# Second stage: down weights of the experts issued by ScalarE on its own DMA queue

## The reference

```
q_emb = relu(cond @ W3 + b3)
h     = relu(((64 * x + sum_over_tokens(x)) * q_emb) @ W2 + b2)
shared = (silu(h @ sw_gate) * (h @ sw_up)) @ sw_down       # inner width 2 * 352 = 704
scores = softmax(h @ gate_w.T); top 6 of 64 experts for each token
each expert takes at most 64 tokens (the first 64 in token order):
    y = (silu(g @ w_gate[e]) * (g @ w_up[e])) @ w_down[e]  # 512 -> 352 -> 512
out   = x + shared + sum over a token's experts of y * score
```

## Time and profile before

| | |
|---|---|
| median of 3 runs | 1211.64 us (1211.52 to 1211.75) |
| profiled execution | 1211.44 us |
| its span | 1209.6 us |
| TensorE busy | 1204.5 us |
| VectorE busy | 857.4 us |
| ScalarE busy | 329.9 us |
| GpSimd busy | 272.9 us |
| DMA, 700 to 800 us | 0.92 of the 16 engines' time, 302 GB/s |
| granted TensorE clock | 1.00 |

### The profile page before, as it was taken

The page is one execution under the profiler, slowest core; times in us unless marked ns, Lnnn a source line. Parts: engine busy times, 40 slices in busy tenths (PEclk is TensorE's granted clock), DMA queues, the critical chain, the costliest instruction groups (busy, mean ns, idle before and its releaser), DMA issues.

```text
span 1209.6 us, 15909 instructions
## 1 busy us (share of the span) xinstructions
PE 1204.5 (100%) x5705; PEld 889.3 (74%) x5705; DVE 857.4 (71%) x1868; ACT 329.9 (27%) x631; POOL 272.9 (23%) x246
## 2 busy tenths in 40 slices
PE   9999999999999999999999999999999999999998
PEld 8888888888888888888866666666666666666666
DVE  7998989988888898886656555664655664655652
ACT  4454243434324353343111111110111201111111
POOL 0000000000000000000136245263463553543421
PEclk9999999999999999999999999999999999999999
DMA  9946444372643626246767988989989889899863
GB/s 220 223 111 192 96 135 118 92 179 52 179 103 85 174 75 158 56 141 200 244 222 248 333 278 271 338 280 276 338 260 327 299 284 307 292 304 301 275 145 87
DMA packets 158999, 250.91 MB, mean 207 GB/s; under 512 B 22664, under 2 KB 93704, under 8 KB 157768
## 3 DMA queue, kind: packets, MB, share of 16 engines
q1 hardware_dynamic: 142528, 222.22, 58.3%
q0 software_dynamic: 14048, 25.18, 10.5%
q10 hardware_dynamic: 2344, 2.50, 0.7%
HBM read 197.14 MB, written 61.10 MB: 213 GB/s over the span
## 4 chain that ended last, share of the span: by engine, by line
PE 95%; DVE 3%; issue 0%; ACT 0%; DMA 0%; DVEq 0%; ACTq 0%
PE bank L1509 23%; PE bank L1510 22%; PE bank L1511 22%; PE bank L1713 13%; PE bank L1728 7%; PE bank L1535 2%; PE bank L1632 1%; PE bank L1631 1%; PE bank L1569 1%; PE bank L1567 1%; PE bank L1580 1%; PE bank L1638 0%; DVE x L951 0%; DVE xpart L955 0%; DVE x L968 0%
## 5 line engine op out<-in xcount | busy, mean ns | idle before, releaser
L1509 PE MATMUL bank<-hh,gu 128*128 128x512 f32 x704 | 278.0, 395 | 0.0
L1510 PE MATMUL bank<-hl,gu 128*128 128x512 f32 x704 | 274.2, 390 | 0.0
L1511 PE MATMUL bank<-hh,gu 128*128 128x512 f32 x704 | 274.1, 389 | 0.0
L629 POOL DMA_INDIRECT hg<-table,idx_quarter x128 | 126.5, 988 | 643.5 <-DVE idx_hi L1391 594.0
L1509 PEld LDWEIGHTS bank<-hh,gu 128*128 128x128 f32 x704 | 132.2, 188 | 39.1 <-issue 12.8
L1511 PEld LDWEIGHTS bank<-hh,gu 128*128 128x128 f32 x704 | 132.2, 188 | 27.8
L1510 PEld LDWEIGHTS bank<-hl,gu 128*128 128x128 f32 x704 | 132.2, 188 | 26.2
L697 ACT ACTIVATE ah<-prod 128x512 fp32r<-128x512 f32 x96 | 60.6, 632 | 302.6 <-DVE prod L1051 287.2
L1468 DVE STREAM_TRANSPOSE eactT<-eact 32x96 f32<-32x96 f32 (+1 forms) x512 | 133.9, 261 | 7.9
L1509 PE MATMUL bank<-sdh,ah 128*128 128x512 f32 x320 | 125.9, 393 | 0.0
L1510 PE MATMUL bank<-sdl,ah 128*128 128x512 f32 x320 | 124.6, 390 | 0.0
(11 more groups left out here) (132 smaller groups left out, 1672.8 us busy)
## 6 DMA issues: line engine op xcount, KB each, us to landing
wg<-in_L_ffn_w_gate_dram SPq DMA_DIRECT2D x64, 704.0 KB
wu<-in_L_ffn_w_up_dram SPq DMA_DIRECT2D x64, 704.0 KB
wd<-in_L_ffn_w_down_dram SPq DMA_DIRECT2D x64, 512.0 KB
table<-hrow SPq DMA_DIRECT2D x64, 256.0 KB, 4.3
x<-in_x_dram SPq DMA_DIRECT2D x60, 256.0 KB, 6.8
wd<-in_L_ffn_w_down_dram SPq DMA_DIRECT2D x64, 192.0 KB
out_dram<-outst SPq DMA_DIRECT2D x35, 256.0 KB
outst<-in_x_dram SPq DMA_DIRECT2D x32, 256.0 KB, 3.5
```

What stands on the lines that cost most here:

```text
L629: nc.gpsimd.indirect_dma_start(out=hg[p % 3][:, b, :], out_offset=None, in_=quarters, in_offset=bass.IndirectOffsetOnAxis(ap=idx_quarter[: ...
L1509: nc.tensor.matmul(o, st_h, mv_h, start=first_mm, stop=False)
L1510: nc.tensor.matmul(o, st_h, mv_l, start=False, stop=False)
L1511: return nc.tensor.matmul(o, st_l, mv_h, start=False, stop=last_mm)
```

## The change

ScalarE issues the down weights of units 1 to 31, on its own queue, after the same semaphore as before and ahead of the SiLU of the unit. SP keeps the down weights of unit 0 (in the first stage, unchanged) and issues gate, up and h as before, on the first queue. Buffers, sizes and semaphores are the same.

```diff
@@ SP's block
-            def load_down(p):
-                wait(sp, s.edown_filled, p)
+            def load_first_down():
                 for e in range(2):
-                    src = w_down[p + NP * e]
+                    src = w_down[NP * e]
                     sp.dma_start(wd[e][:, 0:IT - 1, :],
                                  src[0:(IT - 1) * P, :].rearrange("(i p) d -> p i d", p=P)).then_inc(down_in[e], 16)
                     sp.dma_start(wd[e][0:ITAIL, IT - 1, :], src[(IT - 1) * P:I, :]).then_inc(down_in[e], 16)
...
-            load_down(0)
+            load_first_down()
...
-                if kind == "experts" and 0 < n < NP:
-                    load_down(n)
                 if kind == "experts" and n + 2 < NP:
                     load_gate(n + 2)
                     load_up(n + 2)
@@ ScalarE's block
+            def load_down(p):
+                act.wait_ge(s.edown_filled, p)
+                for e in range(2):
+                    src = w_down[p + NP * e]
+                    act.dma_start(wd[e][:, 0:IT - 1, :],
+                                  src[0:(IT - 1) * P, :].rearrange("(i p) d -> p i d", p=P)).then_inc(down_in[e], 16)
+                    act.dma_start(wd[e][0:ITAIL, IT - 1, :], src[(IT - 1) * P:I, :]).then_inc(down_in[e], 16)
...
                 if kind == "experts" and n < NP:
+                    if n > 0:
+                        load_down(n)
                     silu_expert(n)
```

## The result

The changed kernel takes 1225.53 us (median of 6 runs, 1220.8 to 1231.71), the kernel before 1211.68 (6 runs, 1211.48 to 1212.0). The ratio is 1.0115, 95% interval 1.0083 to 1.0147: slower, by 13.9 us, where 1224.8 had been forecast. The runs spread over 11 us, where the six of before spread over 0.5 us and the 20 that were run beside the first experiments over 2.5 us (1211.27 to 1213.75).

A forecast was written before the change was run, and what follows sets the result against it. TensorE, almost never idle, was taken as the bound. Late down weights in two backlog and six short units add 13.2 us to 1211.44, giving 1224.6, or 1224.8 as median; own range 1215 to 1238, with rivals 1211.3 to 1242.

The forecast's parts named there:

- TensorE has no slack: Whole span: TensorE is busy for all but 5 us of 1209.6, so late weights lengthen the run directly.
- Issuing costs nothing on ScalarE: Four DMA issues ahead of each unit's SiLU: 0 us taken, bounds 0 to 28; up matmuls cover any delay.
- Turns by packet: DMA engines alternate queues per packet; 2 KB down rows beside 5.6 KB rows get about 30% of the time.
- short units: Six units with about 15.8 us between down phases: down weights late by 1.3 us each, bounds 0 and 3.
- GpSimd's store often runs then: In short units the accumulating store adds 19 x 0.17 us, landing at 13.4 us against 13.1 available.
- the working: Down-weight landing from packet turns on a mean engine: 10.2 us after issue usually, 13.4 with the store.
- the last of 16 comes about 1 us later: End of a down transfer: the slowest DMA engine finishes about 1 us after the mean one, an estimate.
- The backlog: Two units issued while large packets still queue: down weights late by 2.7 us each, bounds 0 and 6.
- The sum: Total lateness of down weights over the run: 2 x 2.7 + 6 x 1.3 = 13.2 us, bounds 0 to 30.
- Rival 2: GpSimd's serial scatters, slowed by a third queue, become the bound: +28 us, 1239; chance 0.09 as main term.

The follow-up runs named there:

- the first experiment: Changed kernel with the order restored: SP issues gate and up weights only after the unit's down weights landed, both queues kept; 1212.07 us, ratio 1.0002.
- the exchange: Kernel before, with gate and up weights of units 2 to 31 moved to ScalarE's queue instead of the down weights; 1226.09 us, ratio 1.0115.
- the down-last kernel: Kernel before, one queue, SP issuing each unit's down weights after the gate and up weights of unit n + 2; 1360.53 us, ratio 1.1239.
- the cut store: Changed kernel with GpSimd's two accumulating stores of a chunk's shared part cut from 256 to 32 rows each; 1212.16 us, ratio 1.0008.
- the 4 KB rows: Changed kernel with 256 of each down matrix's 352 rows loaded as 128 pieces of 4 KB instead of 256 of 2 KB; 1216.38 us, ratio 1.004.
- the half-row kernel: Changed kernel with each gate and up matrix loaded in 2.8 KB pieces instead of 5.6 KB, by two DMAs; 1218.28 us, ratio 1.0066.

## Why the prediction was right

- *TensorE has no slack*: right. Waits and clock account for 17.2 of 17.35 us.
- *Issuing costs nothing on ScalarE*: right for the time. The four took from 752.73 to 755.19 in the changed kernel and the SiLU began at 755.29; all on ScalarE gave 1211.73.
- *Turns by packet, for SP's and ScalarE's queues too*: right. That the two kinds of weights must not overlap is shown by the restored order and by the exchange; that they share by turns and not by bytes, by the packet size on either side. The turns are what the Trainium skill, DMA: Bandwidth & Descriptors, section Queues, rings and completion order, states. On its 9 to 17 descriptors in a packet the prediction argued from the equal counts of rows 6; that does not hold, as equal groups on both sides would give equal counts too. The packet records at the end of the unit that landed at 963.85 do tell: its last rows begin in pairs at 961.95, 962.2, 962.5 and 962.8, one about each 0.3 us and not in bursts, which is one row of each queue in turn (0.094 + 0.22).
- *Where*: right in kind (short units and the backlog), wrong in number. Six short units late by 1.3 us were forecast; the trace has three, by 1.3, 4.8 and 1.0 us. Two steps failed. "GpSimd's store often runs then" holds for two of six (in two more it ends within 2.4 us of the issue), and the store was priced too low: the working gives it 19 turns (13.4 us after the issue), but at 834.32 it was issued together with the down weights of 835.01 and ran beside them until 852.1, and they landed after 17.7 us. And "the last of 16 comes about 1 us later" was mis-sized: rows 10, from which it was taken, give 2.4 us (6.5 against 4.1), and in the third late unit, with no store to speak of, the end of the transfer made all of the lateness, landing 14.0 us after the issue where 10.2 was worked out for a mean one. That these add up to 7.1 us against 7.8 is luck.
- *The backlog*: two units of 2.7 us were forecast, one of 4.8 was found (issue 769.94, landed 790.38, so 20.4 us where the working had 17.5 to 18.5). This too comes near by luck: one unit for two, at nearly twice the lateness. The other followed the long wait at 848 to 853, and the time lost there gave its transfer room (852.86 to 873.75).
- *The sum*: 11.9 us of waits against 13.2. That the median came within 1 us of 1224.8 owes much to luck, since a term was missing that is not small: the clock after long waits, 5.3 us in the profiled execution. The prediction put it at nothing without giving a reason. Runs of this one kernel took 1221 and 1232 us. How long the waits of the other runs were was not measured, so that the spread comes from them is an inference.
- *Single landing times* scatter about the working of turns. Of the units without a store beside them some land earlier than the 10.2 us worked out (8.0 us after the issue of 1113.59), one much later (14.0 us); the late ones with a store are 1 to 4 us over. For the changed kernel the two sides nearly cancelled; in the down-last kernel, where nearly every unit was at its limit, the working was 3 us short and the at most 1250 us expected became 1360.5.
- *Rival 2* has not come about (108.1 us of scatter waits against 108.3; last wait for the reload 5.4 against 5.7), but its place is real, as the first experiment's profile shows. The TensorE waits of 1.0 and 1.2 us for gathered rows, in the profiles of the cut store and of the 4 KB rows, are of GpSimd's chain too.

## What to carry to other kernels

Before a transfer is moved to another queue, ask what it was ahead of: here one queue in order of issue was a priority, two queues were none, and the one with the smaller rows lost. If it has to move, hold the less urgent queue back until it has landed, or even out the row sizes. Work out the landing for the last of the DMA engines, not for the mean one. And count a TensorE wait of several microseconds at its length and the slower matmuls behind it.

## What the runs showed of the hardware

- Down weights were slowed by the queues that had work beside them, not by ScalarE's queue as such: with GpSimd's store cut 1212.2 us, with all three queues 1225.5, with all expert weights on ScalarE's queue 1211.7.
- One transfer's end can lie far behind its bulk: 665 of 768 packets through by 956, the last landing at 963.85.
- TensorE's clock went to the lower level within waits of 4.3 to 5.7 us and even 1.2 us after work had begun again behind one of 2.9 us, and stayed there for 3 to 7 us. Near 2.5 us it went both ways: in the half-row kernel waits of up to 2.7 us left it alone (TensorE busy 1204.0 us, as before the change), in the 4 KB kernel one of its waits of at most 2.5 us was followed by down matmuls of 4.49 us, and with the issuers exchanged three of the four waits, of at most 2.9 us, by ones of 4.11 to 4.49 us.
- ScalarE's queue took 2.21 us for one issue of 0.45 us at 835.94, as the SP queue has single ones of 1.3 to 1.5 us before; the SiLU behind it was not late for the up matmuls.
